# ScalarE normalises the tokens instead of GpSimd, GpSimd's long quantisation operations are cut in two, and the planner gets a new table

## The reference

```python
x = x + _L0_attn_a_ref(_layernorm(x), ...)  # band: 16 heads of 64, RoPE, banded softmax, biases
x = x + _L0_ffn_ref(_layernorm(x), ...)     # int8 weights: silu(gate) * up, then down
x = x + _L0_attn_b_ref(_layernorm(x), ...)  # causal: 16 heads of 8, RoPE
x = x + _L0_ffn_ref(_layernorm(x), ...)
x = x + _L1_attn_a_ref(_layernorm(x), ...)  # chunk: 16 heads of 8 in chunks of 64 tokens
x = x + _L1_ffn_ref(_layernorm(x), ...)     # fp4: inputs, hidden values and weights quantised in blocks of 16
x = x + _L1_attn_b_ref(_layernorm(x), ...)  # lowrank: rank-32 projections of q, k, v
x = x + _L1_ffn_ref(_layernorm(x), ...)
```

## Time and profile before

| | us |
|---|---|
| median of 3 runs | 2169.54 (2167.63 to 2172.38) |
| the profiled execution | 2175.12 |
| its span, first to last instruction | 2173.3 |
| TensorE busy | 1791.2 (82%) |
| VectorE busy | 1366.8 (63%) |
| GpSimd busy | 961.6 (44%) |
| ScalarE busy | 803.1 (37%) |

### The profile page before, as it was taken

How to read it: one execution, slowest core, us unless ns; L and a number is a source line. 1 busy time by engine, 2 the same in 40 slices (tenths; PEclk the granted TensorE clock), 3 DMA queues, 4 the chain that set the end, 5 groups by cost and what they waited for, 6 DMA issues and landing times.

```text
span 2173.3 us, 51626 instructions
## 1 busy us (share of the span) xinstructions
PE 1791.2 (82%) x21261; PEld 1259.5 (58%) x21261; DVE 1366.8 (63%) x2749; ACT 803.1 (37%) x1298; POOL 961.6 (44%) x1266
## 2 busy tenths in 40 slices
PE   2899999999999998878999987777776777777774
PEld 2566666666666666655555556666665455555553
DVE  5744445555455553565555555678777688888875
ACT  0233333333333332324444443333433444444442
POOL 1522223333322323443434345589886455555533
PEclk7999999999999999989999999879888788888987
DMA  4000000000000000023333323233332222232210
GB/s 159 1 2 1 1 2 1 1 1 1 1 1 1 2 1 1 16 59 74 70 78 71 77 60 74 46 83 82 79 85 60 59 55 57 64 64 64 58 27 8
DMA packets 167464, 89.54 MB, mean 41 GB/s; under 512 B 9393, under 2 KB 165810, under 8 KB 166978
## 3 DMA queue, kind: packets, MB, share of 16 engines
q1 hardware_dynamic: 167010, 85.70, 17.1%
q0 software_dynamic: 224, 0.54, 0.1%
HBM read 46.36 MB, written 39.85 MB: 40 GB/s over the span
## 4 chain that ended last, share of the span: by engine, by line
PE 48%; DVE 35%; issue 6%; ACT 5%; POOL 2%; DVEq 0%; DMA 0%; POOLq 0%; SPq 0%; ACTq 0%
PE slots L1302 34%; DVE nmx L1194 13%; PE ctx_ps L1302 9%; DVE rope_part L1235 6%; DVE rope_part L1159 2%; PE slots L1577 2%; ACT ctxT L1000 1%; DVE band_r L1160 1%; DVE band_va L626 1%; DVE ctxT L1278 1%; DVE band_va L629 1%; ACT probs L1080 1%; DVE rope_part L1160 1%; ACT band_va L1000 1%; DVE band_va L624 1%
## 5 line engine op out<-in xcount | busy, mean ns | idle before, releaser
L1194 DVE TENSOR_REDUCE nmx<-slots 128x8 f32<-128x1024 f32 (+2 forms) x352 | 407.9, 1216 | 107.9 <-PE slots L1302 104.7
L1080 ACT ACTIVATE probs<-slots 128x1024 f32<-128x1024 f32 (+1 forms) x416 | 356.0, 892 | 302.4 <-PE slots L1302 299.2
L1302 PE MATMUL slots<-band_r 64*64 64x64 bf16 (+4 forms) x5120 | 392.4, 262 | 85.3 <-DVE nmx L1194 42.4
L1302 PEld LDWEIGHTS slots<-band_r 64*128 64x128 bf16 (+2 forms) x5120 | 192.9, 120 | 254.9 <-issue 126.9
L1235 DVE SCALAR_TENSOR_TENSOR rope_part<-slots,bias_qk,rope_band 128x256 f32<-128x256 f32 x512 | 212.3, 477 | 197.4 <-PE slots L1302 173.3
L1302 PE MATMUL ctx_ps<-probs,band_va 64*32 64x64 f32 (+4 forms) x5120 | 257.0, 312 | 47.6 <-issue 24.5
L979 POOL TENSOR_TENSOR band_r<-rope_part 128x512 f32<-128x512 f32 x128 | 164.3, 1284 | 251.0 <-DVE rope_part L1235 251.0
L1302 PE MATMUL slots<-mask,ident_bf 128*128 128x256 bf16 (+1 forms) x896 | 217.0, 324 | 45.9 <-DVE nmx L1194 16.5
L1302 PEld LDWEIGHTS ctx_ps<-probs,band_va 128*32 128x32 f32 (+2 forms) x5120 | 145.4, 118 | 129.8 <-issue 66.0
L893 POOL TENSOR_TENSOR var_eps<-mean_var,eps 128x2 f32<-128x2 f32 x128 | 29.2, 228 | 430.4 <-DVE mean_var L1122 430.4
L1302 PE MATMUL slots<-nmT,pick 64*128 64x256 bf16 (+2 forms) x2560 | 217.6, 240 | 1.5 <-issue 1.4
(11 more groups left out here) (173 smaller groups left out, 2926.9 us busy)
## 6 DMA issues: line engine op xcount, KB each, us to landing
band_r<-scratch SPq DMA_DIRECT2D x192, 192.0 KB, 4.4
scratch<-parts SPq DMA_DIRECT2D x96, 192.0 KB, 2.2
scratch<-parts SPq DMA_DIRECT2D x96, 128.0 KB, 2.1
scratch<-parts SPq DMA_DIRECT2D x96, 64.0 KB, 1.9
x<-in_x SPq DMA_DIRECT2D x16, 128.0 KB, 2.8
out<-x SPq DMA_DIRECT2D x16, 128.0 KB, 1.8
band_r<-in_band_qk_a SPq DMA_DIRECT2D x1, 1024.0 KB, 6.3
band_r<-in_band_qk_b SPq DMA_DIRECT2D x1, 1024.0 KB, 7.9
```

The lines of the kernel that those rows point to most:

```text
L1080: nc.scalar.activation(probs[:, g % 2, step[2], :, 0:width], slot(u, step).rearrange("p (a n) -> p a n", a=2)[:, :, 0:width], ACT.Exp, sca ...
L1194: nc.vector.tensor_reduce(dst, src, axis=AX.X, op=ALU.max, negate=True).then_inc(free_sem(u, step), 1)
L1302: return nc.tensor.matmul(o, lhsT, rhs, start=start, stop=stop, skip_group_check=shared)
```

## The change

- `norm` moves from GpSimd's queue to ScalarE's. It becomes an activation with a scale and a bias for each token, rstd * x + shift, two per norm.
- GpSimd's `root` makes the shift, -mean * rstd, with two more operations on 128 by 2 values, each linked to the next.
- GpSimd's part of the hidden quantisation is issued in two pieces of 352 columns each; the quantisation of tokens and VectorE's part stay whole.
- The waits of `needs()` follow (the bias step waits for ScalarE's norm), the costs of `work()` get other values, and the table `LEAD` and `PER_UNIT` are new. For example, band's maxima on TensorE had a lead of 15.183 against -2.437 for its back stage; they get 51.005 and -26.954.

```diff
-        "st": [("dve", 1.0), ("pool", 0.85)],
-        "xn": [("pool", 0.8)],
+        "st": [("dve", 0.77), ("pool", 1.35)],
+        "xn": [("act", 0.5)],
...
-        "quant": [[("dve", 1.48)], [("dve", 1.93)], [("pool", 4.84)]][i % 3] if name == "quant" else [],
+        "quant": [[("dve", 1.48)], [("dve", 1.93)], [("pool", 5.1)]][i % 3] if name == "quant" else [],
...
-        "parts": [("pool", 1.0)],
+        "parts": [("pool", 1.25)],
...
     "pe": {
-        "tail": {"band": -1.574, "causal": 26.104, "chunk": 10.753, "lowrank": -0.884},
+        "tail": {"band": 4.054, "causal": -0.168, "chunk": 0.879, "lowrank": 2.505},
...
-        "operands": {"band": 4.447, "causal": 7.702, "chunk": 18.901, "lowrank": 57.299},
-        "maxima": {"band": 15.183, "causal": -0.256, "chunk": 0.135, "lowrank": -1.548},
-        "back": {"band": -2.437, "causal": -0.43, "chunk": -0.634, "lowrank": -1.541},
+        "operands": {"band": 31.38, "causal": 0.878, "chunk": 0.532, "lowrank": 0.403},
+        "maxima": {"band": 51.005, "causal": 1.058, "chunk": 0.739, "lowrank": -0.269},
+        "back": {"band": -26.954, "causal": -0.168, "chunk": 45.061, "lowrank": 0.005},
...
-PER_UNIT = 0.01
+PER_UNIT = 0.0012
...
-                lambda: v.tensor_tensor(qx, qx, qp, ALU.add),
-                lambda: v.tensor_tensor(qx, qx, qp, ALU.subtract),
-                lambda: v.tensor_tensor(by_block(dst), by_block(qx), spread(amax), ALU.mult))
+                lambda at, blocks: v.tensor_tensor(qx[:, at], qx[:, at], qp[:, at], ALU.add),
+                lambda at, blocks: v.tensor_tensor(qx[:, at], qx[:, at], qp[:, at], ALU.subtract),
+                lambda at, blocks: v.tensor_tensor(by_block(dst[:, at]), by_block(qx[:, at]),
+                                                   amax[:, blocks].unsqueeze(2).to_broadcast([P, blocks.stop - blocks.start, BLOCK]), ALU.mult))
             for i in which:
-                last = ops[i]()
-                if i < len(ops) - 1:
+                if i < 6:
+                    last = ops[i]()
                     link(last)
+                    continue
+                for k in range(pieces):
+                    part = slice(k * blocks // pieces, (k + 1) * blocks // pieces)
+                    last = ops[i](slice(part.start * BLOCK, part.stop * BLOCK), part)
+                    if i < len(ops) - 1 or k < pieces - 1:
+                        link(last)
...
                     link(nc.gpsimd.tensor_tensor(var_eps[:, b], mean_var[:, b, :, 1], eps[:], ALU.add))
-                    nc.gpsimd.tensor_tensor(rstd[:, b], var_eps[:, b], minus_half[:], ALU.pow).then_inc(rstd_ready, 1)
+                    link(nc.gpsimd.tensor_tensor(shift[:, b], mean_var[:, b, :, 0], minus_one[:], ALU.mult))
+                    link(nc.gpsimd.tensor_tensor(rstd[:, b], var_eps[:, b], minus_half[:], ALU.pow))
+                    nc.gpsimd.tensor_tensor(shift[:, b], shift[:, b], rstd[:, b], ALU.mult).then_inc(rstd_ready, 1)
...
-                    for t in range(TILES):
-                        nc.gpsimd.tensor_scalar(xn[:, t, :], x[:, b, t, :], mean_var[:, b, t, 0:1],
-                                                rstd[:, b, t:t + 1], ALU.subtract, ALU.mult).then_inc(xn_ready, 1)
...
-                                 QUANT_OPS[2]).then_inc(hq_ready, 1)
+                                 QUANT_OPS[2], 2).then_inc(hq_ready, 1)
...
+                    act.wait_ge(rstd_ready, RSTD_NO[u, ahead] + 1)
+                    for t in range(TILES):
+                        nc.scalar.activation(xn[:, t, :], x[:, b, t, :], ACT.Identity, bias=shift[:, b, t:t + 1],
+                                             scale=rstd[:, b, t:t + 1]).then_inc(xn_ready, 1)
```

More of the change, by code:

```diff
@@ L302 @@
+        "operands": {"band": 1.916, "causal": -28.374, "chunk": 0.08, "lowrank": -3.188},
+        "back": {"band": 1.771, "causal": 21.749, "chunk": 35.028, "lowrank": 9.914},
     },
     "dve": {
[L304 to L307 removed]
@@ L316 @@
+        "finish": {"causal": 33.305, "chunk": -12.072, "lowrank": -23.982, "end": -2.254},
+        "forward": {"lowrank": -5.871, "end": -25.776},
+        "operands": {"band": 11.741, "causal": -17.738, "chunk": 1.038, "lowrank": 38.725},
+        "maxima": {"band": 36.891, "causal": -2.596, "chunk": 9.962, "lowrank": -30.825},
     },
 }
-PER_UNIT = 0.01
+PER_UNIT = 0.0012
 def released_by(u, step):
```

80 lines of the change are left out of this document (39 added, 41 removed).

## The result

| | before | after |
|---|---|---|
| median, us | 2170.96 (4 runs, 2167.63 to 2172.39) | 2191.34 (4 runs, 2187.79 to 2193.51) |
| ratio | 1 | 1.0095 (95% interval 1.0078 to 1.0111) |
| span of the profiled execution | 2173.3 | 2186.0 |
| TensorE / VectorE busy | 1791.2 / 1366.8 | 1782.6 / 1360.8 |
| GpSimd / ScalarE busy | 961.6 / 803.1 | 820.6 / 906.4 |

A forecast was written before the change was run, and what follows sets the result against it. TensorE was taken to bind band and causal, VectorE to lead lowrank. Pieces -21, tail +2, norm -3, table 0 gave -22 us: 2175.1 to 2153, less 5.6 for the median, 2147 us; range 2092 to 2207.

The forecast's parts named there:

- part 1: GpSimd's hidden quantisation in two pieces: VectorE gets 1.3 us a lowrank sequence back, -21 us, with +2 in the tail.
- part 2: Norm from GpSimd to ScalarE: shorter path from statistics to tokens, -3 us; ScalarE's idle time hides the added 70 us.
- part 3: The new table holds only the order: nothing booked, gain bounded by TensorE's 44 us idle in band, equal loss possible.
- The reading by stretches: TensorE binds band and causal; GpSimd is busiest in chunk; VectorE is busiest in lowrank and leads its chain.
- The third rival: Norms ahead of exponentials or evacuations freeing TensorE's PSUM slots cost 0.6 us each, 58 us: 2205; this side's chance 0.29.
- The other rivals: More comes back, about 2098, chance 0.19; nothing comes back, 2167, 0.10; Identity needs table loads, 2475, 0.02.
- The signs: Right: three VectorE means 0.7 to 1.2 us, period under 27.5; wrong: TensorE gaps behind norms, band idle above 44 us.

## Why the prediction was wrong, step by step

| step | reckoned, us | measured, us |
|---|---|---|
| part 1, pieces with their tail | -19 | -9.8 |
| part 2, norm to ScalarE, old orders | -3 | +42.2 |
| part 3, table and orders | 0 | -12.8 |
| both of the first together, beyond their sum | - | +0.8 |
| sum | -22 | +20.4 |

The terms depend on the order in which they are taken: with the new orders first, these give 19.4 us and the pieces 2.4.

**What bounds the kernel.** The reading by stretches held for the kernel before. TensorE's waits in band and causal are where the time was lost, and with the pieces alone VectorE's time in lowrank is where it was won. In the changed kernel TensorE leads the chain there.

**Part 1.** The mechanism was right and its size too: 1.27 us of VectorE a sequence against 1.3, pieces of 933 ns against 930, the tail's own price 2.5 against 2. The term that failed is "taken whole since VectorE leads the chain there". The period fell by 0.94 us of the 1.27, and by medians less still. VectorE is busy 83% of this stretch and has about half of its chain; with the pieces TensorE and the exponentials stand where the three operations stood. In the new orders next to nothing of the 1.27 us is left (2.4 us in all, not told from nothing): adding this term to the others was wrong too. The Trainium skill, "SBUF — State Buffer", Terms (shared port pair), says that of VectorE and GpSimd the one that holds this pair holds it for a whole instruction, and the other blocks. The trace agrees in two ways: a wait goes over to the next piece (line 630, 294 to 980 ns), and its length is that of a piece.

**Part 2** is the step that turned the sign: "ScalarE's idle time hides it ... in the sum it is nil". Total idle time was taken for cover. An in-order queue has idle time at certain places, and at the norm's planned place ScalarE came to it 1.2 us before its root started (516.19 and 517.36 us), and stood for the root with a cast behind it that TensorE needed. Moving the norm behind this cast gave back 31 of the 42 us. Two sizes failed too. The norm was priced at 275 ns by a line through two larger operations that read PSUM; it reads SBUF with a scale and a bias for each token, and takes 485. The bias makes 95 of the 210 ns (390 without it). And the four-part root was reckoned to fit in the old path with 0.3 us to spare. It does (2.50 us for 2.73), but a longer root costs all the same: 16 us with the norm left on GpSimd, a part of it because another meeting with VectorE arises. "It was on the chain for a few us only" was read from the waits in one order of work; 0.5 us more of root, 128 times, cost 11 to 24 us wherever it was tried, and the highest figure holds a fall of TensorE's clock.

**The third rival** (ScalarE's queue becomes the wait, 2205, chance 0.29) named the engine, its queue and who pays, and the time of the whole change without its table, 2203, is next to its own. That is luck: its price had another build. It was 16 band norms with 2 us of wait for a cast each, an operand of TensorE and no freed slot, with the clock's answer on top, and not 96 norms with 0.6 us of ScalarE's pair. Its condition was wrong as well: that a norm be ahead of something that frees a slot isn't enough; it must also come to the head of the list before its root is ready. A clue was on record as an idle time: before 69 of the 128 roots GpSimd had nothing to do and started the moment the statistics came (430.4 us before line 893, all of it ended by `mean_var`). For over half of the norms the statistics are late. For the band layer's norms the clue does not hold: there the statistics end at 516.97 us in the timeline of the move alone, and the root starts at 517.36, directly behind GpSimd's own last sum. Both are later than ScalarE's arrival, so what stands in order behind such a norm on a busy engine is held.

**Part 3.** Nothing was booked, within 44 us on either side, and 12.8 us came back with the norm on ScalarE. That is inside the bounds; but as a separate term it doesn't exist, as +232 and +202 us show, and as the 12 us behind the 48th milestone show, which it shares with part 1. A table of priorities that was fitted to a graph is part of that graph.

**The other rivals.** No table load was added: after has one ACT_TABLE_LOAD, as the earlier trace rows. The Trainium skill, "ScalarE: Activation LUTs", Table sets, has identity in every table set. The trace agrees: one load, with 256 of these activations between exponentials.

**The signs.** Means of 0.4 to 0.9 us for the three operations (0.7 to 1.2 foreseen), the gaps of TensorE behind a norm, and 62 us of idle time in the band layer were the signs asked for; the period from the 49th to the 64th milestone, 27.9 us, missed the 27.5 that would have shown the gain of part 1. The last was put down to the table in advance; with the old orders it was worse still, so it is the norm's.

**What stays open.** Why the longer root costs 11 us in the good place: 1.4 of it fall in band, and the chunk layer's share goes with a lower granted clock (0.86 against 0.90 from 1400 to 1600 us). How the 6 us that after keeps without the shift divide between the norm's place and the new orders; in those orders no run took the place alone away. And in which places the 128 longer roots cost their 14 us there: it is spread over three layers, and no single wait shows it.

## What to carry to other kernels

Idle time covers a moved operation only at its place in the queue. Ask when the operation's inputs come, what then stands behind it on its new engine, and who waits for that; give an operation whose inputs come late to an engine on which nothing urgent is queued, or put it behind the urgent work. Cutting an operation that blocks another engine cuts each wait to the length of a piece, and pays until the cutter becomes what is waited for: here two pieces gained 10 us and four lost 12. It also pays only while the blocked engine is what the others wait for: in the new orders the same two pieces gave 2 us that the runs can't tell from nothing. A wait can cost TensorE more than its length, so look at the granted clock before adding up waits. And don't judge a moved step together with a schedule fitted to it: hold the orders fixed for the one, and count the schedule only as what it adds.

## What the runs showed of the hardware

- An activation of 128 x 128 float32 from SBUF takes 485 ns with scale and bias per partition, and 390 with the scale alone; two in a row take 0.86 and 0.69 us. A line through 256 and 1024 columns out of PSUM gave 275.
- An addition or a multiplication of 128 x 2 values takes GpSimd 0.20 to 0.22 us, a power 0.70; a cast of 128 x 64 takes 0.24. Four tiny operations with their links last 1.5 us.
- Cut in two, GpSimd's 704 columns take 2 x 933 ns for 1680, 0.19 us more, as the line through 256 and 704 columns said.
- TensorE's granted clock is full in the band layer of before and of after, with 44 and 62 of 700 us idle, but 0.94 with 63 idle under the new table alone, and 0.98 with 70 idle for the move alone. The sum of idle time doesn't tell it, and a bad order can cost twice: directly behind waits of 2.19 us a pair of products of 128 x 512 took 1.03 us for 0.61.
